# Decoder layer on one core: the vector engine's order in each batch's first step, and the fourth batch's norm one step later

## What is computed

```
x = _layernorm(x + _L0_attn_ref(x, wq, wk, wv, wo), axis=-1)             # 16 heads of 32, 8 kv heads, rope, not causal here
x = _layernorm(x + _L0_xattn_ref(x, ctx_512, Wq, Wkv_expand, Wout), axis=-1)  # 16 heads, causal mask, context of width 128
x = _layernorm(x + _L0_ffn_ref(x, weight1, weight2, weight3), axis=-1)   # silu(x w1) * (x w2), then w3
```

## Time and profile before

| what | us |
|---|---|
| median of 3 runs | 1124.98 |
| lowest, highest | 1119.26, 1127.58 |
| the profiled execution | 1125.64 |
| span of its instructions | 1123.9 |

### The profile page before, as it was taken

The page is one execution under the profiler, slowest core; times in us unless marked ns, Lnnn a source line. Parts: engine busy times, 40 slices in busy tenths (PEclk is TensorE's granted clock), DMA queues, the critical chain, the costliest instruction groups (busy, mean ns, idle before and its releaser), DMA issues.

```text
span 1123.9 us, 17522 instructions
## 1 busy us (share of the span) xinstructions
PE 1038.3 (92%) x6280; PEld 670.4 (60%) x6280; DVE 755.5 (67%) x1560; ACT 482.4 (43%) x587; POOL 439.8 (39%) x462
## 2 busy tenths in 40 slices
PE   9899999999999898998989998998989999999995
PEld 7545455555455454565546556555636888888884
DVE  7778658666866688559676876877673546464535
ACT  3343445554464464546654664676442212112110
POOL 3448675975786564123352432334257000000000
PEclk9899999999999999999989999999989999999998
DMA  6731586386636674646755485757445202011021
GB/s 232 216 91 30 140 220 180 90 242 179 191 84 169 189 203 102 160 92 147 208 140 125 116 202 127 166 147 183 111 135 163 83 1 105 8 38 38 1 75 38
DMA packets 92618, 145.16 MB, mean 129 GB/s; under 512 B 22507, under 2 KB 39795, under 8 KB 92275
## 3 DMA queue, kind: packets, MB, share of 16 engines
q1 hardware_dynamic: 83218, 116.49, 39.8%
q0 software_dynamic: 8000, 26.75, 8.3%
q10 hardware_dynamic: 1312, 0.79, 0.2%
HBM read 78.09 MB, written 23.73 MB: 91 GB/s over the span
## 4 chain that ended last, share of the span: by engine, by line
PE 67%; DVE 19%; issue 5%; DMA 3%; POOL 3%; ACT 2%; SPq 1%; ACTq 0%; DVEq 0%; POOLq 0%
PE att_pv L1041 11%; PE att_scores L978 7%; PE att_scores L1294 7%; PE att_pv L1294 7%; PE att_scores_T L1324 7%; PE att_scores_T L962 6%; PE att_scores_T L1014 5%; PE att_scores_T L964 5%; PE att_scores_T L963 5%; DVE att_mx L1653 4%; PE att_scores_T L1159 2%; DVE att_scores L1648 2%; DVE att_nf_zone L1808 2%; DMA att_nf_home<-nf_reciprocals 2%; DVE att_stats L1684 1%
## 5 line engine op out<-in xcount | busy, mean ns | idle before, releaser
L1461 ACT ACTIVATE att_probs<-att_scores_T 128x1024 f32<-128x1024 f32 (+2 forms) x256 | 218.3, 885 | 161.7 <-PE att_scores_T L1014 159.1
L1041 PE MATMUL att_pv<-att_probs,att_v 128*32 128x512 f32 (+3 forms) x1024 | 216.6, 539 | 7.9 <-POOL att_probs L842 7.1
L1041 PE MATMUL att_pv<-att_probs,att_ones 128*32 128x512 f32 (+3 forms) x1024 | 216.6, 539 | 0.0
L1653 DVE TENSOR_REDUCE att_mx<-att_scores 128x2 f32<-128x1024 f32 x124 | 151.5, 1222 | 86.1 <-PE att_scores L978 85.3
L978 PE MATMUL att_scores<-att_k_stack,att_q_stack 96*128 96x256 f32 (+1 forms) x504 | 168.8, 407 | 32.2 <-DVE att_mx L1653 23.1
L1648 DVE CUSTOM_DVE_ANT_0 att_scores<-att_scores,att_cmask 128x128 f32<-128x128 f32 (+3 forms) x256 | 120.9, 511 | 40.6 <-PE att_scores L978 39.4
L1014 PE MATMUL att_scores_T<-att_q_stack,att_k_stack 97*128 97x512 f32 (+2 forms) x512 | 140.3, 386 | 7.7 <-ACT att_raw L1399 2.3
L978 PEld LDWEIGHTS att_scores<-att_k_stack,att_q_stack 96*128 96x128 f32 x504 | 88.3, 195 | 80.5 <-DVE att_mx L1653 32.8
L842 POOL TENSOR_SCALAR_AFFINE_SELECT att_probs<-att_probs 128x256 f32<-128x256 f32 x128 | 59.0, 461 | 164.8 <-ACT att_probs L1461 159.5
L1014 PEld LDWEIGHTS att_scores_T<-att_q_stack,att_k_stack 97*128 97x128 f32 x512 | 87.7, 195 | 49.4 <-issue 18.9
L1547 ACT ACTIVATE att_probs<-att_scores 128x512 f32<-128x512 f32 x44 | 26.3, 598 | 208.0 <-PE att_scores L1294 208.0
(11 more groups left out here) (262 smaller groups left out, 2102.3 us busy)
## 6 DMA issues: line engine op xcount, KB each, us to landing
att_q_stack<-att_q_hi SPq DMA_DIRECT2D x128, 128.0 KB, 3.2
att_probs<-nf_x SPq DMA_DIRECT2D x28, 352.0 KB, 3.5
att_nf_home<-nf_reciprocals POOLq DMA_DIRECT2D x48, 176.0 KB, 4.8
att_q_stack<-att_q_lo SPq DMA_DIRECT2D x64, 128.0 KB, 3.6
att_k_stack<-att_k_hi SPq DMA_DIRECT2D x64, 128.0 KB, 3.5
att_nf_home<-nf_x SPq DMA_DIRECT2D x20, 352.0 KB, 3.6
w_nf<-att_nf_zone SPq DMA_DIRECT2D x192, 22.0 KB, 2.5
att_k_stack<-att_k_hi SPq DMA_DIRECT2D x64, 64.0 KB, 4.1
```

The lines of the kernel that those rows point to most:

```text
L1041: last = T.matmul(pv[HD * j:HD * j + HD, sums, q0:S], lhs, pr[:, at:at + S - q0], start=(t == 0), stop=(t == TT - 1))
L1461: A.activation(probs_of(b, r)[:, 1024 * h:1024 * h + w], bank[:, 0:w], ACT.Exp, scale=SCALE).then_inc(st_free, 1)
L1653: V.tensor_reduce(mx[:, p % 2, :].rearrange("p (r t) -> p r t", r=2)[:, :, t], sco[:, :, :], AX.X, ALU.max).then_inc(sc_free, 1)
```

## The change

In the first steps with a round (`first`), DVE runs passes 1 and 2 ahead of `sums_of`, and pass 3 directly behind `sums_of`, ahead of maxima 2. The list becomes: maxima 0, maxima 1, passes 1 and 2, sums_of, pass 3, maxima 2, over_sums, scale_rounded, maxima 3. That holds for (2,0), (3,0), (5,0), (6,0) and (7,0). In (1,0) and (4,0), which have no round, nothing moves except that maxima 2 keeps its place.

In batch 3, `begin_spread` goes from (3,3) behind maxima 0 to (3,4) behind maxima 1; `end_spread` from (3,3) behind maxima 1 to (3,5) behind maxima 0; the rows are scaled in two parts in (3,5), two behind maxima 1 and two behind maxima 2, instead of in (3,4) behind maxima 0 and maxima 1. The norms of the other batches stay where they were.

```diff
-                    if b == B - 1 and p == 3:
-                        begin_spread(range(TT))
-                    if (b, p) == (B - 1, 4) or (b, p) == (NB - 1, 5):
+                    if (b, p) == (NB - 1, 5):
                         scale_rows(range(0, 2), TT - 1)
+                    if (b, p) == (B - 1, 5):
+                        end_spread(range(TT))
                     if fore:
                         maxima(*fore, 1)
...
-                    if late(b) and p == 3:
+                    if crossed(b) and p == 3:
                         end_spread(range(TT))
                     if b == B and p == 3:
                         scale_rows(range(TT), TT - 1)
-                    if b == B - 1 and p == 4:
-                        scale_rows(range(2, TT), TT - 1)
+                    if (b, p) == (B - 1, 4):
+                        begin_spread(range(TT))
+                    if (b, p) == (B - 1, 5):
+                        scale_rows(range(0, 2), TT - 1)
...
+                    first = p == 0 and end is not None
+                    if first:
+                        exceeds(end, (1, 2))
                     if p % 2 == 0 and pairs(b, p) > 0:
                         sums_of(G)
+                    if first:
+                        exceeds(end, (3,))
...
-                    if not beside:
+                    if not beside and not first:
                         exceeds(end, (1, 2))
                     if fore and not quick:
                         maxima(*fore, 2)
...
-                    exceeds(end, (1, 2, 3) if beside else (3,))
-                    if quick and b > B and p == 5:
+                    if not first:
+                        exceeds(end, (1, 2, 3) if beside else (3,))
+                    if quick and b > B and p == 5 or (b, p) == (B - 1, 5):
                         scale_rows(range(2, TT), TT - 1)
```

## The result

| | before | after |
|---|---|---|
| median, us | 1122.73 (12 runs) | 1128.69 (12 runs) |
| lowest, us | 1118.79 | 1123.83 |
| profiled execution, us | 1125.64 | 1124.33 |
| its span, us | 1123.9 | 1122.6 |

The account below looks back on a forecast made before the run. TensorE's work (busy 92%) plus its waits bounds the kernel. Terms -0.5 (2,0), 0 (3,0), +2.1 (cross attention), -0.6 (norm) sum to +1.0 us on 1124.98: median 1126.0 us, range 1120 to 1131, no measurable change.

Parts of the forecast that it names:

- (2,0): First step of self attention: rounding product about 1.05 us sooner, next step's product 0.5 us sooner; term -0.5 us.
- (3,0): First step of self attention: -0.5 us locally, hidden behind POOL's chain, so counted 0; up to 0.35 us could be lost.
- Rival D: POOL's chain in (3,0): 0.35 to 1.1 us more, 1126.4 to 1127.1 us; chance 0.62 together with the forecast.
- My dearer price of 1.1 us: In (3,0), by the skill's lock rule, two passes would hold POOL's DMA issue for their whole 1.1 us.
- a longer 1.79 us in (3,1): TensorE's 1.79 us wait in (3,1), for the last part of POOL's weighed values, was to grow.
- Cross attention: (5,0), (6,0), (7,0): maxima 2 falls behind the wait for ScalarE; 0.7 us lost in each, +2.1 us.
- Norm in (3,3): TensorE's 1.21 us wait for maxima 2 is gained in full, and more cannot be.
- Norm in (3,4): maxima 2 comes 0.65 us later relative to the step, leaving some 0.6 of the 1.21 us gained.
- Rival B: Stretches at 1.2 GHz in three first steps of cross attention, 3 x 1.5 us: 1130.5 us; chance 0.13.
- (3,5) and SP's queue: end_spread and rows fit DVE's idle times but for 0.1 us; store and loads 3 us later, costed at nothing.
- rival C: SP's later store makes (3,7) wait for stacks; 5 us beyond the cover give 1131 us; chance 0.03.
- Rival A: Later waits absorb cross attention's losses, the norm gives all its TensorE idle time: -4 us, 1121 us; chance 0.20.

Follow-up runs that it names:

- e5: The changed kernel with cross attention's first steps undone and begin_spread in (3,4) behind maxima 3; 1127.85 us, ratio 1.0024 against the kernel before.
- e9: The kernel before, with all four row tiles in (3,4) scaled behind maxima 1; 1124.20 us, ratio 1.0013.
- e10: The kernel before, batch 3's norm moved to (3,5): begin_spread behind maxima 0, end_spread behind maxima 1, two rows later, two in (3,6); 1120.84 us, ratio 0.9975.
- e12: The kernel before, batch 3's norm moved to (3,5): begin_spread behind maxima 1, end_spread behind maxima 2, two rows later, two in (3,6); 1121.53 us, ratio 0.9973.
- e8: The kernel before, unchanged, timed against itself and profiled again; 1125.16 us, ratio 1.0016.
- e1: The kernel before with the new order only in cross attention's first steps (5,0), (6,0), (7,0); 1125.18 us, ratio 1.0011.
- e2: The kernel before with the new order only in self attention's first steps (2,0) and (3,0); 1124.42 us, ratio 1.0024.

## Why the prediction was right, and where it was not

All twelve kernels and the first comparison can be put into one fit: the time of an execution is the kernel before's in its own comparison, plus a term for each part that its kernel has. By least squares over 283 executions, with 95% intervals (e5's norm and e9's rows have terms of their own, +0.8 ± 2.4 and +1.7 ± 2.2 us):

| part | by the times, us | by its own steps, us | forecast, us |
|---|---|---|---|
| first steps of self attention | +1.9 ± 1.3 | -0.69 in (2,0), +0.85 up to (2,2) | -0.5 and 0 |
| first steps of cross attention | +2.0 ± 1.5 | +1.6 | +2.1 |
| norm as in the change | -0.9 ± 1.4 | +0.35 | -0.6 |
| norm as in e10 and e12 | -3.0 ± 1.5 | -1.5 and -2.2 (against e8) | |

The three parts of the change add up to +2.9 ± 1.5 us (1.86 + 2.01 - 0.94), where +1.0 was forecast. The kernel is a quarter of a per cent slower; the forecast of no change by the bound of 1% holds, and its sign too, but not its size of +1.0. What was mis-sized is the term for self attention's first steps, -0.5 us against a measured +1.9 ± 1.3, and, by the steps, the term for the norm, -0.6 against +0.35. The fit takes the parts as adding up; it doesn't say where in the kernel a part costs its time, and of self attention's +1.9 us only the +0.85 up to (2,2) has a place.

- **(2,0): the step that failed.** The walk through both lists was right to 0.2 us within the step (-0.69 for -0.5, 0.29 us of wait for 0.3). What was wrong is to carry the gain past the step. For (3,0) I had written that whatever TensorE gains there lengthens the wait for POOL. For (2,0) the same chain stood in the same trace, and I didn't follow it, because no row of TensorE named POOL there. Rival D, which I priced for (3,0) alone, belongs to both: the pair of issues grew by 0.13 to 0.26 us in (2,0), which is inside my bound of 0.35. My dearer price of 1.1 us was a wrong use of the rule. It took the issue to wait through both passes; the rows show it held by the first pass alone, and the two begin within 0.12 us of each other and are nearly as long (0.53 and 0.58 us), so little is left to wait.
- **(3,0): right in kind, not provable in size.** (3,0) to (3,2) took 48.45 us on the mean with the new order and 48.15 without, with 45.6 to 52.3 us in single profiles. Nothing of the 0.69 us is left to see. The sign I named, a longer 1.79 us in (3,1), was a bad one: it was 0.23 us after, since the two loads of reciprocals took 6.70 and 8.05 us in that execution, and the one of the earlier trace rows took 9.64.
- **Cross attention: right.** +0.53 us for +0.7 each. DVE waited 2.78 us where I said about 2.4. The part that I had wrong is where TensorE pays (scores behind scale_rounded, not maxima 0).
- **Norm in (3,3): right, and a little more.** -1.5 for -1.21 us, although I had written that it can't be more. The product that waited came 1.38 us sooner from the start of the step (8.67 us for 10.05), not 1.21: the idle time in the bracket of a TensorE row is less than what the wait costs.
- **Norm in (3,4): right but for the clock.** The wait grew by 0.61 us for 0.65. The stretch of 3.4 us at 1.2 GHz behind it costs about 1.6 us (14.90, the mean of the five, less 12.67, the mean of e1, e2 and e8, and 0.61). Rival B had the price right, 1.5 us a stretch, and the place wrong: it looked for stretches in the first steps of cross attention, where none came, though the earlier trace rows showed one in (3,4) itself. A wait that stood in front of a stretch in the profile was the place to ask what happens when it grows.
- **(3,5) and SP's queue: right.** The kernel after scaled two rows in each of the two idle times. end_spread's first instruction, at 443.78, overlapped the end of POOL's memset (443.91) and still took its 0.15 us. (3,5) took 10.21 us for 10.23. SP's store and the loads behind it went out 3.6 to 3.8 us later from the start of the step, and (3,6) to (4,4) kept their lengths to 0.05 us, so rival C had no part. DVE, then SP, in the kernel after:

```profile
446.37 1.00 DVE L1704 TENSOR_SCALAR att_y<-att_y,att_mean_var,att_newton 128x512 f32<-128x512 f32 x2
...
449.59 1.00 DVE L1704 TENSOR_SCALAR att_y<-att_y,att_mean_var,att_newton 128x512 f32<-128x512 f32 x2
```
```profile
450.61 0.39 SPq L577 DMA_DIRECT2D x_after_self<-att_y  x1
451.10 1.98 SPq L491 DMA_DIRECT2D att_q_stack<-att_q_hi  x2
```

- **Rival A: no.** The steps (5,1), (6,1) and (7,1) are as long as before to 0.03 us, so none of the losses in cross attention was taken up there, and the fit has all of it in the total (+2.0 ± 1.5 us). The norm didn't give all of its idle time either.

## What to carry to other kernels

A gain inside a step counts only as far as the next wait for something that doesn't move with it. So follow the load that the next stage waits for back to its issue, in each place where the edit is made, even where the busiest engine's rows don't name it. Work that is moved should go where an engine idles for another reason, past the whole region that is short of it: out of (3,3) into (3,4) it gained nothing certain, out of both into (3,5) it gained 0.27%. And where steps repeat, their lengths, laid side by side over several profiles, resolve 0.1 us where the total scatters by 8.

## What the runs showed of the hardware

- Over 539 executions of all kernels (those of the kernel before counted again in each comparison that used them) the time falls by 1.0 us for each 0.001 that the mean granted clock of TensorE is higher (correlation -0.75, so a good half of the scatter goes with the clock). In the 14 profiles the time at 1.2 GHz adds up to 36 to 60 us: some 20 at the start and the end of the kernel, and nearly all the rest in stretches of 3.4 or 6.8 us, most of them in steps that no edit touches. That these stretches make the scatter, and don't only go with it, is not shown by a run of its own.
- Whether such a stretch comes goes with the wait in front of it in (3,4) (0 of 4, 1 of 4, 6 of 6 above), but not by its length alone: 2.59 us in e5 had none behind it.
- A DVE instruction on four numbers a row with one tensor operand was held by a POOL instruction until that one's end, by a memset (1.77 us in e10) as by a subtraction (1.11 us in e5). One with two was held by POOL's subtractions (2.97 us in the kernel before), and not by a memset (0.16 us beside one in the kernel before, 0.15 us in the kernel after).
- A bf16 pass of 0.58 us on DVE held a DMA issue of POOL until 0.10 to 0.11 us behind its end, in each of seven profiles of (2,0); beside the second pass the next issue took its usual 0.53 us.
